# An FFN over units of 512 tokens, with two attentions beside each, in a fused cross-attention and FFN kernel

## The chip, the cores and the metric

One core of one Trainium2 chip runs the whole kernel. The metric is device time in microseconds. Three runs of the kernel before took 907.23 to 908.13 us, with a median of 907.86 us.

## The reference

The batch has 32 sequences of 128 tokens; x has 256 features and the context 512. All is float32.

```
x = x + xattn(src=ctx, tgt=layernorm(x), mask)     # 8 heads of 32
    src_trans = (ctx @ W_src.T + b_src) * mask     # keys | values, 256 each
    tgt_trans = (tgt @ W_tgt.T + b_tgt) * mask     # queries, 256
    scores    = q k^T / sqrt(32), -inf where the key is masked
    attn      = softmax(scores);  upd = attn v
    out       = concat(tgt, upd) @ W_out.T + b_out
x = x + ffn(layernorm(x))
    h = silu(x W1 s1) * (x W2 s2)                  # 256 -> 1024, ternary weights
    h = gelu(h H1 sh1)                             # 1024 -> 1024
    h = gelu(h H2 sh2)                             # 1024 -> 1024
    out = h W3 s3                                  # 1024 -> 256
```

## The kernel before, in words

The tokens are cut into 16 tiles of 256 (two sequences, NB = 2, T = 256). The FFN weights are ternary, so they are exact in the reduced-precision type fp32r, which the tensor engine takes faster than fp32. An activation is split into a high and a low part of that type (`split`: a copy to fp32r, and the difference), and each product is two matmuls, one for each part, into the same bank. The attention's projections, scores, values and output projection are plain fp32.

In the FFN the features lie on the partitions. Weights of 128 x 128 are the stationary operand and the tile's 256 tokens stream past them (`gate_up`, `middle_steps`, both through `part_product`, L627). Only in the output product (`ffn_out`, L740) the hidden activations are the stationary operand and W3's 256 columns stream. There are four stages: gates (q = 0 to 3, each two blocks of 128 features for gate and for up), first hidden layer (q = 4 to 7), second (q = 8 to 11), output.

While tile f goes through its FFN, the attention of tile f + 1 finishes and that of tile f + 2 begins beside it (`tile(f, a, n, m)` on each engine). On the tensor engine, between gates and first hidden layer stand the key, query and value projections of tile n; between the two hidden layers stand `attend(a)` (probabilities times values), `scores(n)` and `out_proj(a)`. The rest is on the other engines: the scalar engine does silu, gelu and the exponentials; the vector engine masks, takes maxima, normalises, splits and does the layer norms.

Two transposes go by way of memory. The probabilities are transposed in blocks of 32 by the vector engine (`turn_blocks`, L1161), written to `p_dram` (L332) and read back in four pieces (L337); `attend` waits for that. The layer norms' outputs go through `x_dram` and `x2_dram` in the same manner.

Each engine follows its own written order, and semaphores tie the orders together. The order on the sync engine (SP), which issues nearly all transfers, is written out as well. PSUM has eight banks: F0, F1, G0, G1 and the four of S (the scores). A bank holds 128 x 512 values, here two blocks of 256 tokens. Gates and up products go to F and G in turn, the hidden layers to F0 and F1, the attention's products to G.

In the first tile the weights arrive in 22 chunks. Each is looked at by the scalar engine and cast to fp32r by GpSimd (L1459). The loop is over tiles 1 to 12; the first tile and the last three are written out, since they have other neighbours.

## Time and profile before

| | |
|---|---|
| three runs | 907.23, 907.86, 908.13 us |
| span of the profiled execution, first to last instruction | 906.1 us |
| time outside the span, median of the runs less the span | 1.8 us |
| tensor engine busy | 900.6 us (99%) |
| vector engine busy | 615.8 us (68%) |
| scalar engine busy | 390.9 us (43%) |
| GpSimd busy | 76.9 us (8%) |
| matmul instructions | 7600 |

The span is that of one profiled execution. Its own time is not given apart from the span, so it is set against the median of the runs. PE is the tensor engine's matmuls, PEld its weight loads, DVE the vector engine, ACT the scalar engine, POOL GpSimd, SPq the sync engine's queue. Matmuls overlap in the records: what a stream costs is read from the starts of its matmuls or from the length of a group, and not from the duration of one. A fp32 matmul is recorded as two instructions, an fp32r one as one.

### The profile page before, as it was taken

The numbers are of one execution on the slowest core, as the hardware profiler recorded it, in microseconds if no ns is written. First come the engines' busy times: TensorE is split into PE (matmuls) and PEld (weight loads), VectorE is DVE, ScalarE is ACT, GpSimd is POOL, SyncE is SP. The second block draws the span as 40 slices with busy tenths as digits, with TensorE's granted clock in tenths as the row PEclk, the third lists the DMA queues.
The fourth block names the chain that finished last, engine by engine and source line by source line (L and its number), as shares of the span: only waits on it lengthen the run. The fifth ranks groups of instructions, "written<-read, shape, count | busy, mean of one in ns | idle before, by whom it ended". The sixth has DMA issues, their size and how long they took to land.

```text
span 906.1 us, 20825 instructions
## 1 busy us (share of the span) xinstructions
PE 900.6 (99%) x7600; PEld 865.1 (95%) x7600; DVE 615.8 (68%) x1224; ACT 390.9 (43%) x1100; POOL 76.9 (8%) x101
## 2 busy tenths in 40 slices
PE   9999999999999999999999999999999999999998
PEld 8899999999999999999999999999999999999998
DVE  5887858577585776857667586675857857576453
ACT  5872534435253252623525235253443524355231
POOL 3543000010000100001010010100001000000000
PEclk9999999999999999999999999999999999999999
DMA  9932132412314232142311424113241221303000
GB/s 350 382 114 58 60 88 69 122 52 78 84 46 122 58 98 64 40 122 69 112 45 35 122 69 122 35 50 106 69 122 46 72 84 59 94 24 106 24 13 14
DMA packets 82352, 79.27 MB, mean 87 GB/s; under 512 B 8592, under 2 KB 74896, under 8 KB 82320
## 3 DMA queue, kind: packets, MB, share of 16 engines
q1 hardware_dynamic: 81744, 78.31, 28.2%
q10 hardware_dynamic: 576, 0.52, 0.2%
q8 instruction: 21, 0.34, 0.2%
q14 instruction: 11, 0.09, 0.0%
HBM read 51.55 MB, written 27.26 MB: 87 GB/s over the span
## 4 chain that ended last, share of the span: by engine, by line
PE 96%; DVE 1%; DMA 1%; issue 0%; SPq 0%; POOL 0%; ACT 0%; DVEq 0%; POOLq 0%; ACTq 0%
PE F L627 56%; PE G L627 8%; PE F L740 7%; PE G L620 6%; PE G L478 6%; PE G L514 5%; PE G L496 2%; PE S L531 2%; PE G L603 2%; PE F L514 1%; PE S L467 1%; DMA cT<-ctx_t 0%; DMA p_dram<-pb 0%; DMA pr<-p_dram 0%; DVE pr L1107 0%
## 5 line engine op out<-in xcount | busy, mean ns | idle before, releaser
L863 ACT ACTIVATE g<-F,firsts 128x256 f32<-128x256 f32 x248 | 104.0, 472 | 322.9 <-PE F L627 322.7
L627 PE MATMUL F<-hBh,H 128*128 128x256 f32 x1008 | 239.2, 282 | 0.1
L627 PE MATMUL F<-hBl,H 128*128 128x256 f32 x1008 | 236.2, 279 | 0.0
L627 PE MATMUL F<-hAh,H 128*128 128x256 f32 x976 | 231.7, 282 | 0.0
L627 PE MATMUL F<-hAl,H 128*128 128x256 f32 x976 | 228.8, 279 | 0.0
L627 PEld LDWEIGHTS F<-hBl,H 128*128 128x128 f32 x1008 | 190.0, 189 | 0.4
L627 PEld LDWEIGHTS F<-hBh,H 128*128 128x128 f32 x1008 | 188.9, 187 | 0.6 <-ACT g L863 0.3
L627 PEld LDWEIGHTS F<-hAl,H 128*128 128x128 f32 x976 | 183.9, 188 | 0.3
L627 PEld LDWEIGHTS F<-hAh,H 128*128 128x128 f32 x976 | 183.0, 187 | 1.0 <-ACT sil L856 0.4
L1265 DVE CAST hBh<-g 128x512 fp32r<-128x512 f32 x64 | 28.4, 444 | 118.0 <-ACT g L863 117.8
L891 ACT ACTIVATE pr<-pr,nmx 128x128 f32<-128x128 f32 x240 | 92.7, 388 | 0.2
L1267 DVE TENSOR_TENSOR hAl<-g,hAh 128x512 fp32r<-128x512 f32 x128 | 88.7, 693 | 4.4
L1265 DVE CAST hAh<-g 128x512 fp32r<-128x512 f32 x128 | 54.9, 429 | 43.6 <-ACT g L863 42.5
L1431 POOL TENSOR_TENSOR rs<-ve,neg_half 128x2 f32<-128x2 f32 x15 | 10.4, 693 | 648.6 <-DVE ve L1202 648.6
L627 PE MATMUL F<-x2h,W 128*128 128x256 f32 x256 | 61.5, 280 | 0.0
L627 PE MATMUL G<-x2h,W 128*128 128x256 f32 x256 | 61.4, 280 | 0.0
L627 PE MATMUL F<-x2l,W 128*128 128x256 f32 x256 | 61.3, 279 | 0.0
L740 PE MATMUL F<-W,hAh 128*128 128x256 f32 x256 | 61.3, 281 | 0.0
L627 PE MATMUL G<-x2l,W 128*128 128x256 f32 x256 | 61.3, 279 | 0.0
L740 PE MATMUL F<-W,hAl 128*128 128x256 f32 x256 | 61.2, 280 | 0.0
L863 ACT ACT_TABLE_LOAD x17 | 21.8, 1283 | 76.7 <-PE F L627 76.7
L514 PE MATMUL G<-WV,cT 128*128 128x256 f32 x224 | 50.6, 379 | 0.0
(160 smaller groups left out, 1520.0 us busy)
## 6 DMA issues: line engine op xcount, KB each, us to landing
p_dram<-pb SPq DMA_DIRECT2D x30, 512.0 KB, 3.3
pr<-p_dram SPq DMA_DIRECT2D x120, 128.0 KB, 3.2
H_raw<-h SPq DMA_DIRECT2D x16, 512.0 KB, 13.8
cT<-ctx_t SPq DMA_DIRECT2D x14, 512.0 KB, 3.6
x_dram<-xt SPq DMA_DIRECT2D x28, 256.0 KB, 2.4
out<-y SPq DMA_DIRECT2D x32, 128.0 KB, 1.7
x_in<-x_t SPq DMA_DIRECT2D x15, 256.0 KB, 2.7
x2T<-x_dram SPq DMA_DIRECT2D x60, 64.0 KB, 2.0
```

The lines of the kernel that those rows point to most:

```text
L478: ins = mm(k_part(a, c), WK[:, k, c * P:(c + 1) * P], cT_of(a)[:, k, :], start=k == 0, stop=k == KC - 1)
L496: ins = mm(to.rearrange("p (j a i) -> p j a i", j=NB, a=ROWS), WQ[:, k, c * P:(c + 1) * P], turned(xnT)[:, :, k].rearrange("p a j i -> p j ...
L514: ins = mm(v_bank(a)[:, j * D:(j + 1) * D], cT_of(a)[:, k, j * P:(j + 1) * P], WV[:, k, :], start=k == 0, stop=k == KC - 1)
L531: ins = mm(S[:, r, j, c, :], qT[rows, c, j * P:(j + 1) * P], kT[rows, c, j * P:(j + 1) * P], start=True, stop=True)
L603: ins = mm(to.rearrange("p (t b) -> p t b", t=ROWS), v[:, j, h * DH:(h + 1) * DH], pT[j][:, :, r * KD + c, :], start=True, stop=True)
L620: ins = mm(G[1][:, j * D:(j + 1) * D], lhsT, WO[:, k, :], start=k == 0, stop=k == 2 * KD - 1)
L627: return mm(bank, W[0][:, k, cols], part[:, k, :], start=first, stop=last)
L740: ins = mm(F[j][:, 0, :], lhsT, W3[:, k, :], start=first, stop=last)
L863: fn(g[:, q % 2, m, :], mid_bank(f, q)[:, m, :], ACT.Gelu, scale=scols[:, col:col + 1]).then_inc(gelu_ready, 1)
L891: ins = fn(pr[j][:, r, c, :], pr[j][:, r, c, :], ACT.Exp, bias=nmx[:, j, h:h + 1], scale=SCALE, accum_out=den[:, j, h:h + 1])
L1265: V.tensor_copy(hi[:, pair, :], g[:, q % 2, :, :]).then_inc(hi_ready, 1)
L1267: V.tensor_tensor(lo[:, pair, :], g[:, q % 2, :, :], hi[:, pair, :].bitcast(F32), ALU.subtract).then_inc(h_ready, 1)
```

## The change

The 16 tiles are put into nine units. Unit 0 is tile 0 alone, unit u from 1 to 7 is tiles 2u - 1 and 2u together, and unit 8 is tile 15 alone. In a wide unit the gate, up and hidden products stream 512 tokens past each weight block, into one whole bank:

```diff
@@ core of the wide products, TensorE @@
-    cols = slice((2 * q + h) * P, (2 * q + h + 1) * P)
-    ins = ffn_group(gate_bank[:, h, :], (W1, W1_raw), cols, x2h, x2l, general)
+    for k in range(KD):
+        ins = products(gate_bank, (W1, W1_raw), k, cols, x2_parts(k, WIDE), general)
...
+            def middle(u, i, general):
+
+                layer, m = i // KH - 1, i % KH
+                if i == KH:
+                    pe.wait_ge(sil_ready, of_unit("sil_ready", u, KH))
+                elif i == KH + 1:
+                    pe.wait_ge(g_ready, of_unit("g_ready", u, KH))
+                else:
+                    pe.wait_ge(gelu_ready, of_unit("gelu_ready", u, i - KH - 1))
+                for k in range(KH):
+                    if m == 0:
+                        pe.wait_ge(h_ready, of_unit("h_ready", u, KH * layer + k + 1))
+                    ins = products(f_bank(i % 2), ((H1, H1_raw), (H2, H2_raw))[layer], k, slice(m * P, (m + 1) * P),
+                                   h_parts(layer, k, WIDE), general)
+                ins.then_inc(mid_done, 1)
```

The output product stays as it was, one group for each 128 tokens of the unit (j = 0 to 3, banks F0, F1 and two of S). The order on the tensor engine in a wide unit, with a and n the tiles whose attention ends beside it and n and b those whose attention begins (a = 2u + 1, n = a + 1, b = a + 2):

```diff
+            def unit(u, a, n, b, general):
+
+                for m in range(KH):
+                    gate_up(u, m, general)
+                if n is not None:
+                    project_k(n, u)
+                    project_q(n, u)
+                for m in range(4):
+                    middle(u, KH + m, general)
+                attend(a)
+                if n is not None:
+                    scores(n, u)
+                    project_v(n)
+                out_proj(a)
+                for m in range(4, KH):
+                    middle(u, KH + m, general)
+                if n is not None:
+                    project_k(b)
+                    project_q(b)
+                for m in range(4):
+                    middle(u, 2 * KH + m, general)
+                if n is not None:
+                    attend(n)
+                    scores(b)
+                    project_v(b)
+                    out_proj(n)
+                for m in range(4, KH):
+                    middle(u, 2 * KH + m, general)
+                ffn_out(u, TILES - 1 if b is None else b, general)
```

The first unit has two attentions beside its narrow FFN:

```diff
+            def first_middle(general):
+
+                for q in range(4, 8):
+                    middle_pair(0, q, general)
+                scores(2)
+                attend(1)
+                middle_pair(0, 8, general)
+                out_proj(1)
+                project_k(3)
+                middle_pair(0, 9, general)
+                project_q(3)
+                middle_pair(0, 10, general)
+                attend(2)
+                scores(3)
+                out_proj(2)
+                project_v(3)
+                middle_pair(0, 11, general)
+                ffn_out(0, 3, general)
```

The vector engine's order in it, from the end of its first hidden-layer splits, and in a half of a wide unit:

```diff
+                split_pair(0, 7)
+                for j in range(NB):
+                    mask_scores(2, j)
+                    row_max(2, j)
+                bias_v(2)
+                split_pair(0, 8)
+                residual_ln2_stats(1, 0)
+                ln2_apply(1, 0)
+                turn_x2(1)
+                bias_mask_k(3)
+                mask_bias(3)
+                for j in range(NB):
+                    normalise(2, j)
+                    turn_blocks(0, 2, j, "first")
+                split_pair(0, 9)
+                bias_mask_q(3)
+                split_pair(0, 10)
+                mask_scores(3, 0)
+                mask_scores(3, 1)
+                residual_ln2_stats(2, 1)
+                ln2_apply(2, 1)
+                turn_x2(2)
+                bias_v(3)
+                row_max(3, 0)
+                ln1_stats(4)
+                split_pair(0, 11)
+                ln1_apply(4)
+                turn_x(4)
+                row_max(3, 1)
+                x2_lo(1, 0)
+                x2_lo(2, 1)
+                for j in range(NB):
+                    scale_out(0, j)
+                    add_residual(0, j)
...
+            def half_unit(u, layer, p, n, m, slot, home):
+
+                base = layer * KH
+                if n is not None:
+                    bias_mask_k(n, u=u if home == "A" else None)
+                normalise(p, 0)
+                turn_blocks(u, p, 0, home)
+                if n is not None:
+                    mask_bias(n)
+                    bias_mask_q(n)
+                normalise(p, 1)
+                turn_blocks(u, p, 1, home)
+                split(u, base)
+                if m is not None:
+                    ln1_stats(m)
+                split(u, base + 1)
+                if m is not None:
+                    ln1_apply(m)
+                    turn_x(m)
+                split(u, base + 2)
+                split(u, base + 3)
+                if n is not None:
+                    mask_scores(n, 0)
+                    mask_scores(n, 1)
+                    bias_v(n)
+                    row_max(n, 0)
+                residual_ln2_stats(p, slot)
+                ln2_apply(p, slot)
+                turn_x2(p)
+                split(u, base + 4, p)
+                if n is not None:
+                    row_max(n, 1)
+                for i in range(5, KH):
+                    split(u, base + i)
```

The scalar engine in a wide unit; `keep_residual`, a copy of x1, was on the vector engine:

```diff
+            def unit(u, a, n, b):
+
+                for m in range(KH):
+                    silu(u, m)
+                    if m == 0:
+                        keep_residual(u)
+                exps(a, 1)
+                for m in range(4):
+                    gelu(u, KH + m)
+                copy_upd(a)
+                if n is not None:
+                    scale_v(n)
+                    keep_xnT(n)
+                for m in range(4, KH):
+                    gelu(u, KH + m)
+                if n is not None:
+                    exps(n, 0)
+                    exps(n, 1)
+                for m in range(4):
+                    gelu(u, 2 * KH + m)
+                if n is not None:
+                    copy_upd(n)
+                    scale_v(b)
+                    keep_xnT(b)
+                for m in range(4, KH):
+                    gelu(u, 2 * KH + m)
+                x2_hi(u, a, 0)
+                if n is not None:
+                    x2_hi(u, n, 1)
+                    exps(b, 0)
```

What shares a buffer now:

- x2h and x2l, the FFN's input, lie in the last two blocks of hBh and hBl, which the first hidden layer's output fills. `x2_hi` of the next unit so waits for the last middle product of this one (`mid_done`), where before it waited for the last up product.
- pb, the turned probabilities, lie in hB or hA (`pb_of`); `turn_blocks` waits for `mid_done`, and `split` of block 4 waits for `p_written`.
- kT and qT lie in the silu buffer; `bias_mask_k` waits for the unit's eighth product of the gates, and the first silu of the next unit waits for the scores.
- vb is gone: `bias_v` writes v itself and waits for `attend` of the tile before.
- xb is gone, and x_in: x is loaded into xn for the first layer norm, and loaded again into x1 (`reload_x`) for the residual, after the residual copy of the unit; GpSimd adds the bias to it in place.
- `out_proj` writes G0, in which `attend`'s result lies, and waits for its copy (`upd_ready`); before it wrote G1.
- The first k projection of a wide unit waits for the seventh product of the gates, the second one for `bias_v` of the tile before.
- Four outputs of a unit go through two slots of y; the third waits for the first store. The second gate product of a unit waits until all four are scaled.

```diff
+            def reload_x(u, a, slot):
+                sp.wait_ge(res_ready, of_unit("res_ready", u, 1))
+                sp.dma_start(x1[:, slot], x[bass.ds(number(a), 1)].rearrange("o p n -> (o p) n")).then_inc(x1_loaded[slot], 16)
...
+            def scale_out(u, j):
+                dve.wait_ge(out_done, number(outs_before(u) + j + 1))
...
+                dve.wait_ge(stored[j % 2], number((halves_before(u) + j // 2) * 16))
+                V.tensor_tensor(y[:, j % 2, :], out_banks[j][:, 0:D], s3_bc, ALU.mult).then_inc(scaled[j % 2], 1)
```

The last unit is as the last tile was. The loop on the tensor engine is over units 1 to 6; unit 7 has only the attention of tile 15 beside it, and no projections.

## Rows read from the trace of the kernel before

**Rows 1.** The page's head: engines' busy time, and the clock in 40 slices.
```profile
span 906.1 us, 20825 instructions
...
PE 900.6 (99%) x7600; PEld 865.1 (95%) x7600; DVE 615.8 (68%) x1224; ACT 390.9 (43%) x1100; POOL 76.9 (8%) x101
...
PEclk9999999999999999999999999999999999999999
```
**Rows 2.** Busy by stretch: PE, PEld, DVE, ACT, POOL (instructions), clock, DMA.
```profile
60.00:70.00 10.00, 9.08 (x111) 8.52 (x110) 8.46 (x10) 3.40 (x9) 7.21 (x6) 1.00 0.69 201
...
93.20:819.00 725.80, 725.80 (x6174) 701.13 (x6173) 502.69 (x992) 304.37 (x880) 36.14 (x51) 1.00 0.26 77
```
**Rows 3.** Chain of waits over one tile: start us, us, what.
```profile
426.28 1.87 PE G L627 x16
...
433.75 3.45 PE G L478 x16
437.21 1.73 PE G L496 x8
...
442.39 14.93 PE F L627 x128
457.31 1.01 PE G L603 x32
458.33 1.10 PE S L531 x32
459.43 3.65 PE G L620 x16
...
478.02 3.78 PE F L740 x32
```
**Rows 4.** Groups by form: busy us, mean ns of one, idle before.
```profile
L627 PE MATMUL F<-hBh,H 128*128 128x256 f32 x1008 | 239.2, 282 | 0.1
...
L478 PE MATMUL G<-cT,WK 128*128 128x256 f32 x224 | 50.6, 379 | 0.0
...
L627 PEld LDWEIGHTS F<-hBh,H 128*128 128x128 f32 x1008 | 188.9, 187 | 0.6 <-ACT g L863 0.3
```
**Rows 5.** Timeline of DVE in a tile's gates: start us, us.
```profile
428.38 0.88 DVE L1246 SCALAR_TENSOR_TENSOR g<-G,firsts,sil 128x256 f32<-128x256 f32 x2 [0.51 <-PE G L627]
429.29 0.43 DVE L1265 CAST hAh<-g 128x512 fp32r<-128x512 f32 x1
...
430.36 0.87 DVE L1246 SCALAR_TENSOR_TENSOR g<-F,firsts,sil 128x256 f32<-128x256 f32 x2
```
**Rows 6.** Groups of DVE and ACT by form.
```profile
L1107 DVE TENSOR_TENSOR pr<-pr,rden 128x1024 f32<-128x1024 f32 x31 | 38.0, 1225 | 1.1
L1161 DVE STREAM_TRANSPOSE pb<-pr 128x1024 f32<-128x1024 f32 x30 | 37.2, 1241 | 0.6
...
L1193 DVE TENSOR_TENSOR x<-G,xb 128x512 f32<-128x512 f32 x15 | 10.4, 692 | 16.5 <-PE G L620 16.5
...
L891 ACT ACTIVATE pr<-pr,nmx 128x128 f32<-128x128 f32 x240 | 92.7, 388 | 0.2
...
L891 ACT ACT_TABLE_LOAD x16 | 20.5, 1283 | 0.3
```
**Rows 7.** Probabilities' turn and transfers: chain in tile 0, then timelines in tile 7.
```profile
61.66 3.26 DMA p_dram<-pb
...
67.30 2.85 DMA pr<-p_dram
...
445.80 1.25 DVE L1161 STREAM_TRANSPOSE pb<-pr 128x1024 f32<-128x1024 f32 x1
...
447.91 4.31 SPq L337 DMA_DIRECT2D pr<-p_dram  x8
```
**Rows 8.** Timeline of DVE in the first tile, after attend(1).
```profile
70.96 1.22 DVE L1092 TENSOR_TENSOR pr<-S,mbias 128x1024 f32<-128x1024 f32 x1 [0.29 <-PE G L603]
...
74.58 0.69 DVE L1193 TENSOR_TENSOR x<-G,xb 128x512 f32<-128x512 f32 x1 [0.81 <-PE G L620]
...
79.23 0.77 DVE L1237 STREAM_TRANSPOSE xt<-xn 128x256 f32<-128x256 f32 x2
```

More of the change, by code:

```diff
@@ new lines, in unit @@
+            def unit(u, a, n, b, m):
+                reload_x(u, a, 0)
+                if n is not None:
+                    reload_x(u, n, 1)
+                for p, new, after, later, slot, home in ((a, n, b, m, 0, "A"), (n, b, m, None if m is None else m + 1, 1, "B")):
+                    if p is None:
+                        continue
+                    for j in range(NB):
+                        write_p(p, j, home)
+                    for j in range(NB):
+                        read_p(p, j)
+                    if after is not None:
+                        load_mask_row(after)
+                        write_x(after)
+                        if later is not None:
+                            load_x(later)
+                        load_ctx(after)
+                        load_mask_col(after)
+                        read_x(after)
+                    turn_x2(p, slot)
+                store(u, range(4))
@@ L759, in middle_part @@
[L759 to L778 removed]
+                transposes_x(2)
@@ L1325, in tile @@
                     bias_mask_q(n)
-                if a is not None and not early:
-                    normalise(a, 0)
-                if n is not None and not first:
-                    bias_v(n)
-                if a is not None and not early:
-                    turn_blocks(a, 0)
-                if first:
-                    bias_v(2)
-                if a is not None:
-                    normalise(a, 1)
-                    turn_blocks(a, 1)
-                for q in range(4, 8):
-                    split(f, q)
+                normalise(p, 1)
```

955 lines of the change are left out of this document (533 added, 422 removed).

## The prediction

> **What bounds the kernel now.** I read the page's head first, then stretches, the chain of waits over one tile, the groups of matmuls by form, and last the timelines of VectorE and of the queues. The head shows TensorE busy for 900.6 of 906.1 us with the clock at its upper level in every slice [rows 1]. In the loop it is busy for 725.80 of 725.80 us; the only holes are at the two ends, the largest about 1 us [rows 2]. The other engines are hidden. So the change is worth what it takes from TensorE's stream, less what it makes TensorE wait.
>
> The chain for one tile has a period of 55.5 us: 64 gate and up products at 1.87 us per 16, 256 middle ones at 14.93 per 128, 32 output ones in 3.78, and the attention's projections, scores, values and output projection [rows 3]. An FFN matmul over 256 tokens thus starts every 14.93/128 = 116.7 ns. At 2.4 GHz 256 columns are 106.7 ns, so 10 ns of each are not columns. The fp32 projections, also 256 columns wide but slower through the array, start every 3.45/16 = 215.6 ns, and one of their matmuls lasts 379 ns where an FFN one lasts 282; the weight loads of the FFN last 187 ns and are busy nearly throughout [rows 3, 4]. I read that as a weight load that just fails to fit under a 256-column stream.
>
> **The change: TensorE's stream.** Seven pairs of tiles run their gate, up and middle products over 512 tokens: 320 matmuls per unit in place of 640, 2240 in all. The output matmuls have the tokens as weights and stay 256 columns wide (64 per unit at 118 ns), and the attention's matmuls stay as they are. The trace has no FFN matmul over 512. From below, 512 columns at 2.4 GHz are 213.3 ns. From above, if the 116.7 is a rate and not a load, it is 233.3. The nearest row is the fp32 one, whose pace is 215.6 with a weight load in each; I take 215.7. Gain: 2240 x (233.3 - 215.7) = 39.4 us, with ends 0 and 44.8.
>
> The Trainium skill ("TensorE: Matmul & The Clock Gate", back-to-back issue gap) gives N/2.4 + 2.5 ns once warm. For 512 that is 215.8, which my value is near; for 256 it is 109.2, and this trace has 116.7. If the rule held at both widths doubling would gain 2.5 ns per pair, 5.6 us; but the old side is measured, so the measurement decides.
>
> **Loop units (six).** Work per unit beside PE: two attentions, as before, and the FFN's copies in pieces of 128x512. I walked the order with these durations.
>
> Gates: TensorE needs 8 x 1.73 = 13.8 us. VectorE's round for two 256 pieces is 430.36 - 428.38 = 1.98 us [rows 5]. One 512 piece in place of the pair (0.88) costs between 0.69, the nearest 128x512 row [rows 6], and 0.88; I take 0.75, so the round is 1.85. The first product can start at 1.96 after the gates begin, the seventh is ready at 1.96 + 6 x 1.85 + 0.75 = 13.81, and the next k projection waits for it on TensorE with everything behind it: 0.05 us late with the signal. The two ends of the piece's cost move it by -0.4 to +0.9.
>
> Turned probabilities, first half, in us from the start of the gates. The eighth split ends at 1.96 + 7 x 1.85 + 1.93 = 16.8. Then in VectorE's order: k's bias, for which k(n) ends at 17.3 (to 18.25); normalise and turn of the first batch, 1.45 and 1.25 with the small reciprocal in it [rows 6] (to 21.0); the mask and q's bias, 1.1 (to 22.05); normalise and turn of the second (to 24.75). From the end of such a turn (447.05) to the end of the last read's issue took 5.2 us and a last landing some 2.85 more, 8.0 in all [rows 7], so 32.8. TensorE wants it after k (3.45), q (1.73) and four middle groups of 16 x 0.2157 = 3.45, at 13.85 + 5.2 + 13.8 + 0.55 for the first batch = 33.4: hidden by 0.6 us. Before, the same data landed at 455.1 and attend began at 457.31 [rows 3, 7], over 2 us of cover. Second half, from the start of the second layer: both exps (8 x 0.386 each, and 1.28 for the table [rows 6]) now stand behind the last gelu of the first layer, which ends 4.3 us before that point. They end at -4.3 + 1.3 + 6.2 = 3.2, normalise and turn of the second batch at about 6.8 (q's bias between), the landing at 14.8; TensorE wants it at 13.8 + 0.55. Late by 0.4 us.
>
> What waits behind attend is TensorE alone, and all of it: the matmuls are in one queue, so each late landing is paid in full.
>
> The eight output sums have two slots in y, so the third waits for the first store; it is scaled about 0.5 us after the output matmuls end and the gates want the bank at 1.73: hidden. The x2 copies wait for the last middle matmul and take 3.4 us beside 7.55 of output matmuls: hidden. The residual copy goes to ScalarE (two of 0.6) between two silus and fits; the x reload is 14 transfers on queues that are idle most of the time. On SP the reload stands ahead of the writes and reads of the probabilities and waits for the residual copy, done 3 us into the gates, long before them. Together (0.05 + 0.4) x 6 = 2.7 us; bounds 0 and, if each half is 1.5 us late, 18.
>
> **First unit.** It now holds the attention of tiles 1 and 2, where the first tile held one. Before, attend(1) waited until its transfers ended (61.66 to 70.15 [rows 7]) and took 0.7 more. ScalarE is full there and gets the residual copy: 0.5 us later, 71.4. From there TensorE goes through a middle pair (3.73), out_proj(1) (3.65, to 78.8), k of tile 3 (3.45), a pair, q (1.73), a pair, 20 us of work, and wants tile 2's probabilities at 71.4 + 20.0 + 1.0 + 0.55 = 93.0; the 1.0 is k(3)'s wait below. VectorE, in order from 71.4: the rest of split 7 (1.0), masks and maxima of tile 2, four at 1.22 and two small (5.3), stretched by an estimated 1.4 beside the last four weight casts on GpSimd (to 79.1), bias_v (0.7, to 79.8: k(3) wants its bank at 78.8 and waits 1.0), a split (1.1), the layer norm of tile 1 from residual to turn (74.58 to 79.99, 5.4 [rows 8], to 86.3), k's bias and the mask (1.0), twice normalise and turn (5.4). That ends at 92.7, and 8.0 more make 100.7: TensorE idle for 7.6 us. Even with no stretch and no split in it the order needs over 20 us before the transfers start. Then tile 2's x2 hangs on VectorE: from the end of attend(2), out_proj(2) ends at 4.8, then stand the layer norm (5.5), bias_v (0.7), a maximum (1.4), tile 4's statistics (1.35), the last split (1.1), tile 4's apply and turn (1.55), a maximum (1.4), two x2 copies (1.4): 19.2, against 15.8 on TensorE (scores 1.1, out_proj 3.65, v 3.45, a pair 3.73, output 3.78): 3.4 late. ScalarE's exps of tile 3 are still behind that, so the first silu of unit 1 is late, 2.1. (ScalarE: tile 2's x2 copy 16.8, table 1.3, exps 3.1, table 1.3, silu 0.7, so 23.2 where 21.2 was wanted.) Sum 0.5 + 1.0 + 7.6 + 3.4 + 2.1 = 14.6. Below, a quarter less of VectorE's work gives 7; above, 20.
>
> TensorE has had no idle time like 7.6 us in this trace, and its clock never fell [rows 1, 2]. If it falls to 1.2 GHz after it, the 12 us that follow cost up to double; bounds 0 and 12, I take 1.5, nearer to the row.
>
> **Seventh unit and last.** The seventh has no next projections, so tile 15's probabilities (30.2) are wanted at 28.2: 2.0; and out_proj waits for the copy of the bank that it now shares, 0.7. The last tile alone is as before.
>
> **Sum.** -39.4 + 2.7 + 14.6 + 1.5 + 2.7 = -17.9. From a span of 906.1 that is 888.2; the median of the runs shown, 907.9, lies 1.8 above the span, so 890.0.
>
> **Rivals.**
> *A, the first unit is hidden better* than I walked it (transfers faster than 8.0, VectorE less stretched) and the clock stays: the 16.1 us of it shrink to nothing, 873.9. For it: before, the same corner cost TensorE 1 us only. Against: the sum of VectorE's rows alone is above TensorE's.
> *B, the loop's covers are gone*: 0.6 and -0.4 us are thin, and a transfer beside reloads may be 1.5 us longer. 12 halves x 1.5 = 18 instead of 2.7: 905.3.
> *C, the 10 ns is a fixed price per matmul*: 223.3 each, gain 22.4, result 907.0, no change. Against: the fp32 stream pays 2.3 over 512 cycles [rows 3].
> *E, the clock falls in the 7.6 us* and the 12 us after it run at 1.2 GHz: 12 instead of 1.5, 900.5. For it: no row has so long a hole. Against: 1 us holes left the clock alone [rows 2].
> *D, the other side: the array takes fp32r columns at 116.7 per 256.* Then 512 cost 233.3, nothing is gained, and the waits stand: 907.9 + 21.5 = 929.4. With my waits it turns the result to slower from 17.9/2240 = 8.0 ns above my value, 223.7 ns. For it: weight load and matmul keep one pace, which can't tell who leads. Against: 280 cycles for 256 columns is no natural rate, as the fp32 stream shows.
>
> The Trainium skill ("TensorE: Matmul & The Clock Gate", HAM oscillation) says that TensorE goes back to half rate over long idle gaps, which is E; no row of this trace shows it.
>
> **Chances.** My own case 0.56 (880 to 900), A 0.17, B 0.10, E 0.06, C 0.05, D 0.06. Range 872 to 906: it takes in A, E and most of B, and leaves C in part and D out. Measurement can tell 0.2%, 1.8 us. Faster 0.88 (mine, A, E, most of B), same 0.04, slower 0.08.
>
> **What would show it.** Right: wide matmuls starting every 215 to 217 ns; a loop period of about 106 us for two tiles; one hole of 5 to 9 us near 92 to 100 us before attend(2), a second of 3 before unit 1. Wrong: 223 or more between wide matmuls; holes in each loop unit of over 1 us at the values product; a slice with a lower clock.

## The result, and the profile after

The changed kernel takes 942.75 us (median of 4 runs, 941.95 to 944.0) against 907.82 for the kernel before on the same chip: a ratio of 1.0384, with a 95% interval of 1.0369 to 1.0399. The forecast was 890.0 (872 to 906), faster. It is slower by 34.9 us, and the time lies outside the range.

The page's head, and below it stretches in the columns of [rows 2]:

```profile
span 940.2 us, 15690 instructions
...
PE 910.7 (97%) x5360; PEld 764.4 (81%) x5360; DVE 603.5 (64%) x1152; ACT 374.2 (40%) x946; POOL 80.4 (9%) x101
...
PEclk9998799999999999999999999999999999999999
```
```profile
70.00:80.00 10.00, 4.59 (x40) 4.22 (x37) 9.72 (x13) 0.60 (x1) 5.95 (x6) 0.66 0.22 66
93.20:110.00 16.80, 10.46 (x104) 8.82 (x104) 8.13 (x12) 2.76 (x6) 0.00 (x0) 0.70 0.52 149
...
140.00:820.00 680.00, 673.42 (x3765) 556.16 (x3764) 453.62 (x851) 264.33 (x664) 38.53 (x49) 1.00 0.27 79
```
TensorE has 2240 matmuls fewer and yet is busy 10.1 us longer than in [rows 1], and idle 29.5 us where it was idle 5.5. Weight loads did become rarer, PEld fell from 95% to 81%; nothing came of it. The clock is no longer at its upper level everywhere.

The chain of waits over one unit of two tiles, columns as in [rows 3]:

```profile
353.18 0.44 DVE y L1545
...
354.14 3.51 issue
...
357.94 0.76 DVE g L1504
...
369.95 3.72 PE G L595 x16
...
375.40 14.91 PE F L753 x64
...
458.73 3.79 PE F L891 x32
...
467.30 3.52 issue
```
64 wide products take 14.91 us, 233 ns each: what 128 narrow ones took in [rows 3]. And in each unit of the loop the chain leaves TensorE for 3.5 us of "issue" on VectorE, time in which that engine waited for nothing that the profile shows. TensorE then stands still for 0.94 us before a gate product and for 0.61 us before the k projection. From one such stretch to the next are 113.16 us, for two tiles that took 111.0 before.

TensorE's timeline where it waited over 1 us in the first unit (the bracket is the idle time before, and what ended it):

```profile
71.34 0.64 PE L730 MATMUL G<-pr,v 128*32 128x128 f32 x16 [1.24 <-DMA pr<-p_dram]
76.16 0.79 PE L753 MATMUL F<-hB,H 128*128 128x256 f32 x2 [4.17 <-POOL H L1783]
...
102.64 1.08 PE L730 MATMUL G<-pr,v 128*32 128x128 f32 x16 [4.87 <-DMA pr<-p_dram]
105.20 1.08 PE L730 MATMUL G<-pr,v 128*32 128x128 f32 x16 [1.47 <-DMA pr<-p_dram]
...
126.57 0.72 PE L753 MATMUL G<-hB,W 128*128 128x512 f32 x2 [2.71 <-DVE hB L1469]
```
Behind the second, the fourth and the fifth, and behind `attend(15)` in the seventh unit, the clock is at its lower level (1.2 GHz, 0.50 in the clock's column), and TensorE is busy throughout:

```profile
76.20:79.40 3.20, 3.20 (x15) 3.20 (x16) 3.13 (x4) 0.00 (x0) 1.87 (x2) 0.50 0.00 0
105.20:110.00 4.80, 4.80 (x52) 3.89 (x53) 1.63 (x2) 0.60 (x1) 0.00 (x0) 0.50 0.03 8
127.40:130.60 3.20, 3.20 (x9) 2.48 (x8) 0.59 (x2) 3.18 (x13) 0.00 (x0) 0.50 0.49 153
837.50:840.50 3.00, 2.98 (x7) 2.46 (x8) 0.00 (x0) 0.00 (x0) 0.00 (x0) 0.50 0.00 0
```
With the 1.1 us of `attend(2)` between its two waits and the ends of these stretches, TensorE worked some 16 us at half speed, which costs 8.0.

### The profile page after: what moved, and what is told of

The parts are those of the page before. It is cut to its first block, busy times and chain, and to the rows that moved or that the text cites. A ratio compares the mean times of both kernels' runs of the same rounds, so it can differ in the third digit from the quotient of the medians.

```text
span 940.2 us, 15690 instructions
## 1 busy us (share of the span) xinstructions
PE 910.7 (97%) x5360; PEld 764.4 (81%) x5360; DVE 603.5 (64%) x1152; ACT 374.2 (40%) x946; POOL 80.4 (9%) x101
## 4 chain that ended last, share of the span: by engine, by line
PE 83%; issue 4%; DVE 4%; ACT 4%; DMA 3%; SPq 1%; POOL 1%; DVEq 0%; ACTq 0%; POOLq 0%
PE F L753 49%; PE G L742 6%; PE G L595 5%; PE G L635 5%; PE G L753 5%; PE F L891 3%; PE S L891 3%; PE G L617 2%; PE S L655 2%; DVE g L1504 2%; PE G L730 1%; ACT look_out L1169 1%; ACT pr L1110 1%; DMA pr<-p_dram 1%; SPq L416 1%
## 5 line engine op out<-in xcount | busy, mean ns | idle before, releaser
L753 PE MATMUL F<-hB,H 128*128 128x512 f32 (+1 forms) x1120 | 243.5, 377 | 4.2 <-POOL H L1783 4.2
L753 PE MATMUL F<-hA,H 128*128 128x512 f32 (+1 forms) x1088 | 237.9, 378 | 0.6 <-issue 0.4
L753 PEld LDWEIGHTS F<-hB,H 128*128 128x128 f32 x1120 | 196.9, 190 | 45.2 <-POOL H L1783 4.4
L753 PEld LDWEIGHTS F<-hA,H 128*128 128x128 f32 x1088 | 191.1, 188 | 42.0 <-issue 0.8
L1083 ACT ACTIVATE g<-F,firsts 128x512 f32<-128x512 f32 x112 | 77.1, 688 | 325.4 <-PE F L753 325.3
L1538 DVE TENSOR_TENSOR hA<-g,hA 128x512 fp32r<-128x512 f32 x112 | 77.6, 693 | 3.9
L753 PE MATMUL G<-hB,W 128*128 128x512 f32 (+1 forms) x288 | 67.2, 376 | 6.5 <-DVE g L1504 3.8
L753 PE MATMUL F<-hB,W 128*128 128x512 f32 (+1 forms) x288 | 65.9, 373 | 0.0
L753 PEld LDWEIGHTS F<-hB,W 128*128 128x128 f32 x288 | 49.7, 190 | 11.6 <-DVE g L1504 1.5
L595 PE MATMUL G<-cT,WK 128*128 128x256 f32 x224 | 51.1, 382 | 2.8 <-DVE g L1504 2.8
L1738 POOL TENSOR_TENSOR rs<-ve,neg_half 128x2 f32<-128x2 f32 x16 | 12.6, 788 | 422.1 <-DVE ve L1282 421.5
L1133 ACT ACTIVATE v<-v,mcol 128x256 f32<-128x256 f32 x30 | 13.6, 500 | 69.8 <-DVE v L1324 69.8
```

The costliest lines, as they stand in the source:

```text
L595: ins = mm(k_part(a, c), WK[:, k, c * P:(c + 1) * P], cT_of(a)[:, k, :], start=k == 0, stop=k == KC - 1)
L753: ins = mm(bank, W[0][:, k, cols], part, start=start, stop=stop)
L1083: fn(wide_g(i), f_bank(i % 2), ACT.Gelu, scale=scols[:, KH + i:KH + i + 1]).then_inc(gelu_ready, 1)
L1538: V.tensor_tensor(lo[:, m, :], wide_g(i), hi[:, m, :].bitcast(F32), ALU.subtract).then_inc(h_ready, 1)
```

## The experiments

Times are medians; behind each stands its ratio to the kernel before, with the 95% interval. The kernel before, run beside them, was at 907.40 to 907.96. "Less" and "more" are against the changed kernel, or against the kernel that is named. Two theories stood at first for the lost 39.4 us. *Columns:* the array takes fp32r columns at one pace, whatever the width (the forecast's D). *Fixed price:* a matmul pays for its columns and a little more, and something in the kernel takes the gain away. For the rest there were the loop, the first unit's order, and the clock.

**m1: streams alone.** Nothing of the reference is computed; 64 products of one form in a row, then the next form.

```diff
+            def r256():
+                for i in range(64):
+                    mm(banks[1][:, 0:256], w_r[:, i % 8, :], x_r[:, i % 2, 0:256], start=i == 0, stop=i == 63)
```


> A kernel that does none of the reference's work: only streams of matmuls on TensorE, 64 each (fp32 32), with nothing else running: fp32r with 128, 256, 384, 512 columns and eight weight blocks in turn, fp32r 512 with one block always, bf16 with 128, 256, 512, fp32 with 256, 512. Theory W (fp32r columns pass at 116.7 ns per 256, 0.456 per column): starts every 116.7 at 256, 175 at 384, 233.3 at 512, also with one block; bf16 512 at 213 to 216. Rival L (a weight load of about 117 ns is the floor, columns at 0.417): 117 at 128 and at 256, 160 to 163 at 384, 214 to 216 at 512. Rival M (the other engines' traffic in the full kernel slows the stream): alone, 109 at 256 and 216 at 512.

The timeline, the first row of each stream (fp32r 128, 256, 384, 512, 512 with one weight block; bf16 256, 512; fp32 256):

```profile
25.17 5.03 PE L60 MATMUL bank<-x_r,w_r 128*128 128x128 f32 x44
...
32.26 7.89 PE L64 MATMUL bank<-x_r,w_r 128*128 128x256 f32 x64
...
39.99 0.35 PE L68 MATMUL bank<-x_r,w_r 128*128 128x384 f32 x1
...
51.09 9.27 PE L72 MATMUL bank<-x_r,w_r 128*128 128x512 f32 x40
...
65.64 4.70 PE L76 MATMUL bank<-x_r,w_r 128*128 128x512 f32 x20
...
83.73 6.50 PE L84 MATMUL bank<-x_b,w_b 128*128 128x256 bf16 x58
...
90.72 9.45 PE L88 MATMUL bank<-x_b,w_b 128*128 128x512 bf16 x43
...
104.53 5.78 PE L92 MATMUL bank<-x_f,w_f 128*128 128x256 f32 x26
```
From start to start by 64: fp32r 110.8 ns at 128, 120.8 at 256, 173.4 at 384, 227.3 at 512; bf16 109.2 and 215.8. The bf16 stream takes (215.8 - 109.2)/256 = 0.416 ns a column, and so does the fp32r stream from 256 up. So fp32r has a fixed price of some 14 ns a matmul over its 256 or 512 columns. With one weight block it is no cheaper (226.7), but the trace has a weight load for each matmul there too, so that stream does not tell what a load costs. The widths tell more: 256, 384 and 512 columns lie on one line, so the floor that holds 128 columns at 110.8 is not what prices the wider ones. Alone, doubling gains 14.3 ns a pair. None of the three theories fits. And 120.8 and 227.3 differ from the kernels' own 116.7 and 233.3, in opposite senses. The Trainium skill ("TensorE: Matmul & The Clock Gate", back-to-back issue gap) has N/2.4 + 2.5: 109.2 and 215.8, which is the bf16 stream exactly and not the fp32r one.

**e1_narrow: each wide product as two of 256 columns.**

```diff
-                for k in range(KH):
...
+                for half in range(2):
+                    for k in range(KH):
```


> The changed kernel with each product over 512 tokens issued as two matmuls over 256, one half of the bank after the other; buffers, order and all else as in the changed kernel. Theory W: the wide stream gave nothing, so the time stays within 1.5 us of the changed kernel's 942.8. Rival L or M (wide matmuls do save something that other losses hide): 2240 pairs cost what they had saved, at 8 ns a pair 18 us more, 960 or above.

968.29 us, 1.0673 (1.0656 to 1.0689). It could not decide: TensorE's loop body is now long, and at each of its five back edges TensorE itself stands still in two waits of 1.4 to 2.5 us, 19.5 in all over the five. Each pair has half clock behind it. The page's queues show what it waits for, 75 fetches of instructions on q8 where the changed kernel had 20:

```profile
q8 instruction: 75, 1.23, 0.6%
```
**e2_dve_unrolled: VectorE's loop written out.**

```diff
-            with dve.Fori(1, LAST - 2) as i:
-                unit(Count(i, 1, 0), *(Count(i, 2, n) for n in (1, 2, 3, 4)))
+            for i in range(1, LAST - 2):
+                unit(i, *(2 * i + n for n in (1, 2, 3, 4)))
```


> The changed kernel with VectorE's loop over units written out (five units), the other engines' loops as they were. Theory B (the back edge of VectorE's loop costs 3.9 us of fetching, since the body no longer fits where it is kept; TensorE loses 1.55 us at each of four): the holes before the first gate product go and the time falls by 6.2 us, to 936.5. Rival (something else delays that product, the silu or the stores, and the hole is only where VectorE waits): no change, or under 1 us.

933.16 us, 1.0275 (1.0261 to 1.0289), 9.6 less, where 6.2 was expected. The chain is TensorE alone, and its period is 462.38 - 351.35 = 111.03, twice 55.5:

```profile
351.35 1.86 PE G L753 x8
...
371.46 14.94 PE F L753 x64
...
462.38 1.86 PE G L753 x8
```
The loop had four back edges, (113.16 - 111.03) x 4 = 8.5 us; the expectation had counted only the two holes of TensorE at each. The half clock behind `attend(15)` stayed away too (1.7), and the first unit ended 0.6 later. In the changed kernel VectorE stood still at each back edge while its instructions were fetched; three 8 KB fetches lie in the 12 us around one (first fence: the transfers of that stretch; second: VectorE's timeline):

```profile
q14 instruction: 3, 0.02, 0.8%
```
```profile
357.94 0.75 DVE L1504 SCALAR_TENSOR_TENSOR g<-G,firsts,sil 128x512 f32<-128x512 f32 x1 [3.87 <-issue]
```
From 200 to 700 us q14 has 22 fetches, 9 with the loop written out, and none in the kernel before, whose body is one tile. The Trainium skill ("Runtime: NRT & Kernel Launch", instruction fetch mechanics) says that a taken branch whose target is outside the small window of held instructions must fetch it before going on; the trace agrees, at 3.9 us on VectorE.

**e4_casts_first: the first unit's order.** VectorE's layer norm of tile 3 stands behind the maxima of tile 2, and GpSimd's last weight casts ahead of its part of that norm.

```diff
                 split_pair(0, 7)
...
                 bias_v(2)
+                ln1_stats(3)
+                ln1_apply(3)
+                turn_x(3)
@@ GpSimd @@
-                if n == EARLY + KH + 4:
-                    inverse_std1(3)
                 cast(n)
...
+            inverse_std1(3)
```


> The changed kernel with the first unit's order changed on VectorE and GpSimd alone: the layer norm of tile 3 comes behind the masks of tile 2, so that the eighth split, and the last weight casts that wait for it, come earlier. Theory C (the 4.2 us hole at 72 us is the second layer's first product waiting for those casts, and a lower clock follows it): the hole shrinks to under 1 us, the clock stays up there (1.7 us), what hangs behind comes 3 us or more sooner: 936 to 938. Rival (the attention of tile 2 sets the end of the first unit in any case): the hole moves to attend(2), change under 1.5 us.

939.76 us, 1.0348 (1.0334 to 1.0363), 3.0 less: the wait of 4.2 us for the casts is 2.3, and the stretch of half clock around it is 3.4 us long where it was 6.8. That is less than the theory wanted and more than its rival. The changed kernel's chain runs through tile 3's layer norm (xn), then a split (hB), then the last two casts of H2, which wait for that split:

```profile
69.96 2.15 DVE xn L1289 x2
...
73.32 0.70 DVE hB L1519
74.08 2.04 POOL H L1783 x2
```
 With the norm moved, the split still waits 1.4 us for the scalar engine's gelu, and the two casts, 2.0 us, come after it; this is what remains.

**e5_casts_and_unrolled: both.**

> The two single edits together: VectorE's loop written out, and the first unit's order of VectorE and GpSimd turned round so that the weight casts are not behind tile 3's first layer norm. Alone they gave -9.6 and -3.0 us against the changed kernel's 942.75. Theory 'two separate causes': 930.2, the loop units free of holes, the hole before the first product of the second layer at 2.3 us. Rival 'they share time' (the first unit's late VectorE feeds the loop's holes): 932 to 933, as the written-out loop alone.

928.59 us, 1.0237 (1.0219 to 1.0256): 14.2 less, slightly more than the sum of 12.6. They are two causes.

**e6_and_no_transfer.** Instead of writing and reading tile 2's probabilities, SP only waits for them and frees `attend`.

```diff
-                write_p(2, j, "first")
-            for j in range(NB):
-                read_p(2, j)
+                sp.wait_ge(pb_ready, at("pb_ready", 1, j + 1))
+                sp.sem_inc(p_written[j], 16)
+                sp.sem_inc(p_loaded[j], 64)
```


> As the kernel before it in this job (VectorE's loop written out, casts ahead of tile 3's layer norm), and the transfer of tile 2's turned probabilities to memory and back in the first unit is left out, so that attend(2) reads what lies there: tile 2's attention isn't the reference's. Theory 'the two holes before attend(2), 5.1 and 1.7 us, are the transfer, and the stretch of half clock of 10.2 us behind them hangs on them': the holes go, and half of 10.2 us with them; 6.8 + 5.1 = 11.9 us less, 918. Rival 'the x2 wait takes it': TensorE comes earlier to the second unit's gates, VectorE does not, and the 2.7 us hole there grows by most of the 6.8: 4 to 6 us less, 924 to 926.

922.39 us, 1.0156 (1.0138 to 1.0174): 6.2 less than e5, about half of the theory's 11.9. A wait of 2.0 us before attend(2) stayed where none was expected: what is left is VectorE's turn itself, which SP still waits for. The x2 wait, 2.7, did not grow, so that rival fell; but the stretch of half clock at it is 6.8 us long where it was 3.4, which takes back part of what the other stretch gave (10.2 to 3.4).

**e7_narrow_no_loops: e1 made clean,** with TensorE's and VectorE's loops written out.

```diff
-                with pe.Fori(1, LAST - 1) as i:
-                    unit(Count(i, 1, 0), *(Count(i, 2, n) for n in (1, 2, 3)), general)
+                    for i in range(1, LAST - 1):
+                        unit(i, *(2 * i + n for n in (1, 2, 3)), general)
```


> The changed kernel with VectorE's loop written out, and each 512-column product as two products of 256 into the halves of the same bank, with TensorE's loop written out too, so that its longer body isn't fetched anew at the back edge: 2240 fp32r matmuls more, and 2240 weight loads more. Theory 'in the kernel 512 columns cost exactly two times 256': 933.2, as the same kernel with wide products, within 2 us, and no holes in the units. Rival 'the wide products do save what they were made for, 14 ns a pair by the micro kernel': 933.2 + 2240 x 14.3 ns = 965. Rival 'half a bank later each copy': the wait for a whole bank is the same in both, so nothing.

935.73 us, 1.0304 (1.0282 to 1.0325), 2.6 more than the same kernel with wide products, where the saving of the micro kernel would make it 32 more. In its chain 128 narrow products take what 64 wide ones do:

```profile
373.14 14.93 PE F L753 x128
```
So in this kernel, as it lies in memory, width gains nothing. Why does it alone?

**m2_layouts.** The reference's work is left out again. Weights and activations have the kernel's shapes, and neighbours run beside the last three streams.

```diff
+                order = [(k, part) for k in range(8) for part in parts]
+                for i, (k, part) in enumerate(order):
+                    ins = mm(bank[:, 0:width], W[:, k, m * P:(m + 1) * P], part[:, k, 0:width], start=i == 0, stop=i == n - 1)
```


> This leaves all of the reference's work out: it is streams of fp32r products alone, eight accumulation groups in each, with the kernel's layout of weights (a slice of 128 columns of [128, 8, 1024]) and its high and low parts. Streams: 256 columns; 512 columns; 512 with the high part alone (each weight block used once); 512 with all high parts ahead of all low parts; 512 with each product a group of its own; then 512 as in the kernel while VectorE reads and writes SBUF, while ScalarE reads PSUM, and while transfers write SBUF. In the first of these micro kernels 512 columns started every 227.3 ns and 256 every 120.8; in the changed kernel they start every 233.3 and 116.7. Theory 'the layout or the pairs set it': the plain 512 stream is at 233.3 here and 256 at 116.7, and one of the variants (one part, in turn, own groups) is at 227. Rival 'the neighbours take it': the plain stream is at 227 and one of the last three is at 233 or more. Rival 'it is neither, but the rest of the kernel (its values, its power, its clock)': all eight are at 227 and 256 at 120.8.

The four streams of 512 that run alone are at 226.7 to 226.9 ns, and 256 columns at 120. Beside VectorE, the scalar engine or transfers most gaps at full clock are 226 or 227 ns as well. The third answer, then: something that this kernel's layout still lacked. Single matmuls told more than means. In m2 nearly every gap was 226 or 227 ns; in the changed kernel most run from 230 to 236. The kernels have a line that m2 has not:

```
PAD = 8
...
        sb("pad", [P, PAD])
```
It stands ahead of the FFN's activations. By the order of the declarations it puts them 32 bytes past a multiple of 256 from the weights, in both kernels. In m1 and m2 the two have the same address to a multiple of 256.

**m3_addresses.** Streams alone, the moving operand at several byte addresses.

```diff
+            def moving(k, at_byte, width):
+                at = at_byte // 4 + k * 512
+                return h[:, at:at + width]
```


> This leaves all of the reference's work out: nineteen streams of 33 fp32r products alone, each with another byte address of the moving operand (0, 4, 16, 32, 48, 64, 96, 128 bytes past a multiple of 128, 512 columns; five of them at 256; two at 128) and four with the weights 32 bytes past it. Both micro kernels before had every operand at a multiple of 128 bytes and gave 226.7 ns per 512 columns and 120.8 per 256; the two kernels under study have a pad of 8 floats ahead of the FFN's activations, so that these lie 32 bytes past a multiple of 64, and gave 233.3 and 116.7. Theory 'the address of the moving operand sets it': 512 columns take 226.7 at 0, 64 and 128 and 233.3 at 32 and 96; 256 columns 120.8 and 116.7. Rival 'the weights' address': only the last four streams differ. Rival 'neither': all at 226.7 and 120.8.

The numbers fit none of the three. 512 columns took 231.0 to 233.9 ns with the moving operand 0, 16, 32, 48, 64 and 96 bytes past the start of its array, 239.5 at 4, and 226.8 at 128; with the weights moved by 32 it was 233.3. By the order of the declarations that start lies 128 bytes from the weights, to a multiple of 256, so the fast stream is the one at distance 0. That suggests the distance between the two operands. It does not exclude the moving operand's own address to a multiple of 256: the weights were moved only where the stream was slow anyway.

**e8_pad_16, e9_pad_16_and_both, b0_before_pad_16.** 64 bytes in place of 32: in the changed kernel, in e5, and in the kernel before.

```diff
-PAD = 8
+PAD = 16
```


> The changed kernel with a pad of 16 floats in place of 8, so that the activations lie at a multiple of 64 bytes. Theory 'the address': 2240 wide products at 226.7 in place of 233.3, -14.9 us; the 512 narrow ones of the first and last unit at up to 4 ns more, +2: 930. Rival 'the waits take it' (a faster TensorE comes earlier to what VectorE and the transfers bring): half of it, 936. Rival 'the address does nothing': 942.7.

> VectorE's loop written out, the casts ahead of tile 3's layer norm, and the pad of 16. Without the pad's change 928.6. Theory 'the address' with no waits behind it: 928.6 - 13 = 915.7. Rival 'the waits take it': the loop units, whose period is then 106.7 us of TensorE, show holes before the values product, 920 to 925.

> The kernel before with the pad of 16 and nothing else. Theory 'the address, and 256 columns take it the other way': 4608 gate, up and middle products at 120 in place of 116.7, +15 us: 923. Rival 'only 512 columns depend on it': 907.7.

e8: 930.82 us, 1.0261 (1.0243 to 1.0280), 11.9 less for one number. e9: 918.92, 1.0138 (1.0116 to 1.0160), 9.7 less than e5, between its two theories, and no loop unit has a hole before the values product. b0: 906.17, 0.9983 (0.9973 to 0.9993), where 923 was expected. The wide products of e8 are at 14.67/64 = 229.2 ns:

```profile
372.67 14.67 PE F L753 x64
```
The 930 expected for e8 was met by luck: the wide products gave some 9 us and not 14.9. What made up for it is that the output products got cheaper (113 to 115 ns) where narrow products were to get dearer, and that the half clock behind `attend(15)` stayed away. The narrow kernel did not get dearer either. Its hidden layers went up to 117.8 ns; its gates came down to 113 to 114, and so did its output products:

```profile
477.21 3.64 PE F L740 x32
```
So 64 bytes are not what m1 and m2 had, a miss that the next runs answer in part.

**m4_distance.** Streams of 33, the distance from weights to moving operand in bytes.

```diff
+            def m512_32():
+                for i in range(33):
+                    ins = mm(banks[1][:, 0:512], weights(i), moving(i % 8, 32, 512), start=i == 0, stop=i == 32)
```


> This leaves all of the reference's work out: twenty streams of 33 fp32r products alone, with the kernel's stride of weights and the moving operand 0, 32, 64, 96, 128, 160, 192, 224, 256, 384, 512 and 1024 bytes past the weights' address in steps of 256 (512 columns), and the first eight of these at 256 columns. In the micro kernel of addresses 512 columns took 226.8 ns where both operands had the same address to within a multiple of 256 bytes, and 231 to 240 elsewhere. Theory 'the distance of the two operands, to a multiple of 256 bytes': 226.7 at 0, 256, 512 and 1024, 231 to 234 at all others; 256 columns 120.8 at 0 and 117 to 119 at the others. Rival 'a multiple of 128 will do': 226.7 at 128 and 384 as well. Rival 'it was the stride of the weights': all alike.

Timeline, first rows: 512 columns at distances 0, 32, 64, then 256 and 384; then 256 columns at 0, 32, and 192, 224:

```profile
42.81 7.42 PE L65 MATMUL bank<-h,W 128*128 128x512 f32 x32
...
50.29 7.86 PE L70 MATMUL bank<-h,W 128*128 128x512 f32 x33
...
57.99 2.24 PE L75 MATMUL bank<-h,W 128*128 128x512 f32 x9
...
65.56 4.84 PE L80 MATMUL bank<-h,W 128*128 128x512 f32 x20
...
104.09 6.29 PE L105 MATMUL bank<-h,W 128*128 128x512 f32 x27
...
111.58 7.86 PE L110 MATMUL bank<-h,W 128*128 128x512 f32 x33
...
134.26 4.12 PE L125 MATMUL bank<-h,W 128*128 128x256 f32 x33
...
138.21 2.05 PE L130 MATMUL bank<-h,W 128*128 128x256 f32 x16
...
157.73 2.45 PE L155 MATMUL bank<-h,W 128*128 128x256 f32 x20
...
161.49 4.06 PE L160 MATMUL bank<-h,W 128*128 128x256 f32 x33
```
From start to start by 33: 512 columns take 226.7 ns at 0, 233.3 at 32, 229.4 at 64, 227.0 at 256. By single matmuls 96, 128, 160, 192, 224 and 384 are all at 233 to 234, and 512 and 1024 at 226.7 to 227.4. The theory's pattern stands for 512 columns, and "a multiple of 128" falls. 256 columns go the other way: 119.7 at 0, 118 at 32, 113.9 at 192. Only the moving operand was shifted, so for 512 columns distance and its own address are still not told apart. For 256 columns they are: W3, which streams in the output products, has one address in the kernel before, in b0 and in b1, and its products take 118, 113.8 and 120 ns as the other operand moves.

**e10_same_address, b1_before_same_address.** Distance 0 in e5 and in the kernel before.

```diff
-PAD = 8
+PAD = 64
```


> VectorE's loop written out, the casts ahead of tile 3's layer norm, and a pad of 64 floats: the activations then have the weights' address to within a multiple of 256 bytes. With the pad of 8 this kernel took 928.6, with 16 (64 bytes off) 918.9. Theory 'distance': wide products at 226.7 each, 2240 x 6.6 = 14.9 us less than with 8, 913.7; the 800 or so narrow ones of the two end units and of the output at up to 3 ns more, so 914 to 916. Rival 'the waits take it': as with 16, 919.

> The kernel before with the pad of 64 floats, so that operands have one address to within 256 bytes. Theory 'distance': its 5120 narrow products of 256 columns at 120 to 121 in place of 116.7, +15 to +20 us: 923 to 928. Rival 'only 512 columns depend on it': 906 to 908.

b1: 924.37 us, 1.0182 (1.0165 to 1.0199), the dear side for narrow products, as forecast; they are at 119.9 ns:

```profile
449.52 15.35 PE F L627 x128
```
e10: 918.49 us, 1.0133 (1.0109 to 1.0156), where 914 to 916 was expected. The wide products did come down to 226.9:

```profile
363.77 14.52 PE F L753 x64
```
The 2240 are 13.6 us shorter than in e5. Some 2.3 go to the narrow ones and the output's, at 119.9 where they were 117 and 118.3, and the two waits of attend(2) grew from 4.9 and 1.2 to 5.8 and 1.9, since TensorE came earlier and the transfer did not.

**e11_probabilities_sooner: e10 with another first unit.**

```diff
                 turn_x(3)
+                for j in range(NB):
+                    normalise(2, j)
+                    turn_blocks(0, 2, j, "first")
+                residual_ln2_stats(1, 0)
...
                 split_pair(0, 8)
-                residual_ln2_stats(1, 0)
...
@@ ScalarE @@
-                gelu_pair(0, 8)
                 exps(2, 0)
+                exps(2, 1)
+                gelu_pair(0, 8)
```
and on SP the probabilities' transfer stands ahead of tile 1's `turn_x2`.

> As e10, and the first unit's order changed so that tile 2's probabilities come sooner: ScalarE's exponentials of tile 2 ahead of the gelu of the first product pair of the second layer, VectorE's normalising and turning of them ahead of tile 1's second layer norm, and the transfer ahead of that norm's. Theory 'the hole before attend(2) is the order on VectorE and ScalarE': normalise starts at about 81 where it started at 88.4, the data land at 92 where they landed at 99.6 and 101.9, the two holes of 4.9 and 1.2 us go, and part of the stretch of half clock behind them; 6 to 10 us less than e10, 905 to 908. Rival 'the layer norm of tile 1 is then late for q(3) or x2': a new hole of 2 to 4 us before the q projection of tile 3 or before unit 1, 909 to 912.

909.12 us, 1.0020 (1.0010 to 1.0029), 9.4 less than e10, within the 6 to 10 forecast, though just above its 908. In the chain `attend(2)` follows the middle products without a gap:

```profile
91.48 3.83 PE F L753 x32
95.31 1.01 PE G L730 x32
```
The waits of 7.7 us and the stretch of half clock behind them are gone, and no new wait came. Together the edits win back 33.6 of the 34.9 us, the address with them. The wide kernel is then about as fast as the narrow one was (907.84), and no faster.

**b2_narrow_192, b3_narrow_192_both.** The kernel before, put on the cheap side: PAD = 48; and PAD = 16 with W3, which streams in the output products, moved as well.

```diff
+        sb("pad3", [P, 32])
         W3, W3_raw = with_raw("W3", KH, D)
```


> The kernel before with a pad of 48 floats: its activations then lie 192 bytes past the weights' address in steps of 256. In the micro kernel of distances 256 columns took 113.9 ns there, 119.8 at 0 and 117.4 to 119.6 elsewhere, and in the kernel before with a pad of 16, where the output products have W3 192 bytes past the activations, these took 113.8. Theory 'distance': 4608 gate, up and middle products at 113.9 in place of 116.7, 12.9 us less: 895, which beats both kernels. Rival 'the pattern over weight blocks differs in the kernel from that of the micro kernel': 903 to 908.

> The kernel before with a pad of 32 floats ahead of W3 and one of 16 ahead of the activations: these are 192 bytes past the weights of the gates and the hidden layers as in the kernel before it in this job, and W3, which streams in the output products, is 192 bytes past the activations. Theory 'distance': 512 output products at 113.8 in place of 118, 2.1 us less than that kernel: 893. Rival: W3's move changes nothing, 895.

b2: 907.29 us, 0.9979 (0.9956 to 1.0002). Its eleven executions fall on two levels with nothing between, four at 901.4 to 901.9 and seven at 907.1 or over. b3: 899.30 us (898.54 to 900.12), 0.9911 (0.9895 to 0.9926), the fastest kernel here, but not as expected. The first and the second hidden layer, with equal distances, differ:

```profile
438.09 15.08 PE F L628 x128
...
458.93 14.53 PE F L628 x128
...
473.46 3.77 PE F L741 x32
```
The gates (1.81 us per 16) and one layer are at 113.1 to 113.5 ns, the other layer stays at 117.8, and the output products, the only ones that b3 moved against b2, did not get faster (117.8). b2 and b3 missed their 895 and 893. So away from distance 0 the distance, to a multiple of 256, does not fix the pace of a narrow product. What chooses its levels stays open.

## Why the prediction was wrong

*Stream.* The term -39.4, "I take 215.7", failed, and with it the result. 512 columns took 233.0 to 233.4 ns, the upper bound of that step, and the gain was nothing: without its back edges the loop takes 111.03 us for two tiles (e2), twice the 55.5 of [rows 3]. Two things were mis-sized. The fp32r stream pays about 13.4 ns for a matmul of 512 columns even in the best case (m1, m2, m4), where I let the fp32 row stand for it, with its 2.3. And some 6.5 ns of each wide product hung on a pad of 8 floats (e5 against e10). My reading, "a weight load that just fails to fit", is refuted as the price: a load that just fails to fit under 256 columns fits under 512, and the fixed price is the same 14 ns at both (m1). The forecast gave D 0.06 because 280 cycles for 256 columns looked unnatural. The 116.7 was a mean over single gaps of 113 to 120 ns, which the trace of before would have shown. Why the address counts stays open.

*Why D's figure but not its reason.* In the kernel as changed, 512 = 2 x 256 (e7), as D says. At distance 0 it is 226.9 against 2 x 119.9 = 239.8, in the manner of C's fixed price. C's number, 223.3, was the nearest to the 226.7 that is the best any wide stream showed here.

*Loop units.* 2.7 was forecast, for late probabilities; measured are 8.5, for something else. The covers that I called thin held: no loop unit waited before `attend` (rival B fell). The back edge of VectorE's loop was not among my steps (e2).

*First unit.* 14.6 was forecast, and the new waits are 4.2 + 4.9 + 1.5 + 2.7 = 13.3. The x2 wait (3.4) was 2.7 and the one before attend(2) (7.6) was 6.3. The 4.2 for the weight casts was no step of mine: the last casts of H2 wait for a split that stood on VectorE behind tile 3's layer norm (e4, which took 1.9 of it away). The delay of 1.0 at k(3) and the late silu of 2.1 did not appear. That the total came near to 14.6 is luck in part: the waits that I had named came to 9.1.

*Clock.* I took 1.5, "nearer to the row", and E had 0.06; some 8.0 were lost. No row gave the 1.5 or E's 12 us. E's mechanism was right, and it was not one place but four. The argument against it, that holes of 1 us left the clock alone, says nothing of holes of 4. Nor does it hold for all short ones: the two of 1.2 and 0.9 us at `attend(15)` had half clock behind them in the changed kernel and none in e2. What decides there, no run shows.

*Seventh unit.* 2.7 forecast, 1.2 + 0.9 + 0.2 = 2.3 measured.

Sum: 0 + 8.5 + 13.3 + 8.0 + 2.3 = 32.1 of the 34.1 by which the spans differ; 2.0 stay unassigned. The waits that I had priced at 20.0 came to 24.1. The 39.4 that they were to be paid from was not there.

## What to carry to other kernels

A gain that is a difference of two paces needs both paces measured on the same type, at the same addresses: one stream alone would have cost less than the whole change. Look at single gaps before reading a mean as a rate; gaps that vary over products of one width say that something beside the width sets them. When a loop's body is made longer, put its back edge on every engine among the costs, and when a stretch gains an idle time of several us, price the clock behind it.

## What the hardware showed that I had not expected

- The pace of an fp32r stream depends on where its operands lie: 512 columns took 226.7 to 227.4 ns when weights and moving operand had the same address to a multiple of 256 bytes, and 229 to 239.5 otherwise (m3, m4). 256 columns go the other way: 119.8 there, 117.4 to 119.8 at most other distances, 113.9 at 192. Why, and what chooses among the levels of the narrow ones in a kernel (113 to 114 or 117 to 118), stays open. One number in a pad moved the wide kernel by 11.9 us and the narrow one by 16.5.
- The same program can run at two paces: b2 at 901.4 to 901.9 us or at 907.1 and over, with a granted clock of 1.00 in nine of its eleven executions, the four short ones among them. No run here tells what chooses.
- A loop with a body of two tiles stalled VectorE 3.9 us at each back edge, and e1's, the longest on TensorE, stalled that engine some 3.9 us (19.5 over five); written out, both stalls were gone (e2, e7).
